# A graph-attention layer on one core: the last group of rows closed over three tiles and written out by itself

## What is computed

```python
h = jnp.maximum(_layernorm(x, axis=-1), 0.0)
h = h @ W.T                                   # 4096 x 256
src, dst = h @ a1, h @ a2
e = jax.nn.leaky_relu(src[:, None] + dst[None, :], negative_slope=0.2)
e = jnp.where(adj == 0, NEG_INF, e)           # adj is 4096 x 4096
out = x + jax.nn.softmax(e, axis=1) @ h
```

## Time and profile before

| what | value |
|---|---|
| median of three runs | 390.85 us |
| lowest and highest | 390.27, 391.11 us |
| profiled execution, its own time | 390.91 us |
| its span, first to last instruction | 389.3 us |
| mean granted TensorE clock | 1.000 of full speed |

### The profile page before, as it was taken

The page is one execution under the profiler, slowest core; times in us unless marked ns, Lnnn a source line. Parts: engine busy times, 40 slices in busy tenths (PEclk is TensorE's granted clock), DMA queues, the critical chain, the costliest instruction groups (busy, mean ns, idle before and its releaser), DMA issues.

```text
span 389.3 us, 9291 instructions
## 1 busy us (share of the span) xinstructions
PE 380.9 (98%) x3368; PEld 330.9 (85%) x3368; DVE 367.0 (94%) x476; ACT 196.7 (51%) x282; POOL 43.4 (11%) x73
## 2 busy tenths in 40 slices
PE   6999899999999999999999999999999999999996
PEld 5788588888888888888888888888888888888885
DVE  4999999999999999999999799999988999999965
ACT  5899956553345643444445543444345543444330
POOL 2898002000000001110000001100000011100000
PEclk9999999999999999999999999999999999999999
DMA  8920177876559567776666567766665567776403
GB/s 254 372 78 3 38 245 221 272 226 232 176 172 293 181 212 225 240 229 219 223 215 219 174 217 230 237 222 220 216 207 178 165 215 243 228 222 223 152 0 108
DMA packets 26108, 77.89 MB, mean 200 GB/s; under 512 B 2916, under 2 KB 8552, under 8 KB 26088
## 3 DMA queue, kind: packets, MB, share of 16 engines
q1 hardware_dynamic: 24528, 74.20, 58.9%
q0 software_dynamic: 1280, 3.16, 2.2%
q10 hardware_dynamic: 280, 0.26, 0.2%
HBM read 73.40 MB, written 4.21 MB: 199 GB/s over the span
## 4 chain that ended last, share of the span: by engine, by line
PE 87%; DVE 8%; ACT 2%; issue 1%; DMA 1%; SPq 0%; ACTq 0%; DVEq 0%
PE ps L1278 86%; DVE stats L733 2%; DVE hnt_lo L752 1%; DVE v_sb L765 1%; DMA x_sb<-x 1%; DVE rows_sb L1128 1%; DVE moments L737 1%; ACT c_row L493 0%; DVE first_lo L752 0%; ACT h_sb L465 0%; ACT hn_sb L472 0%; DVE hn_sb L760 0%; ACT hnt_hi L482 0%; PE ps L1216 0%; DVE shift L747 0%
## 5 line engine op out<-in xcount | busy, mean ns | idle before, releaser
L1278 PE MATMUL ps<-v_sb,p_hi 128*128 (+2 forms) x2048 | 252.8, 272 | 1.4 <-ACT p_hi L503 1.4
L513 ACT ACTIVATE p_hi<-p_sb,gp 128x1024 f16<-128x1024 f32 x126 | 144.4, 1149 | 167.7 <-DVE p_sb L793 138.8
L1278 PEld LDWEIGHTS ps<-v_sb,p_hi 128*128 128x128 f16 x2048 | 198.3, 97 | 30.1 <-ACT p_hi L503 1.5
L800 DVE SCALAR_TENSOR_TENSOR p_lo<-p_sb,gp,p_hi 128x1024 f16<-128x1024 f32 x126 | 160.3, 1275 | 9.0 <-ACT p_hi L513 8.8
L793 DVE SCALAR_TENSOR_TENSOR p_sb<-c_row,gp,adj_sb 128x1024 f32<-128x1024 uint32 (+1 forms) x126 | 160.1, 1275 | 0.0
L1278 PE MATMUL ps<-v_sb,p_lo 128*128 (+1 forms) x1024 | 141.3, 273 | 0.0
L1278 PEld LDWEIGHTS ps<-v_sb,p_lo 128*128 128x128 f16 x1024 | 99.6, 97 | 13.5 <-DVE p_lo L786 0.3
L449 POOL DMA_DIRECT2D out<-rows_sb x24 | 13.0, 541 | 260.8 <-DVE rows_sb L1095 260.8
L390 POOL TENSOR_SCALAR hn_sb<-x_sb,moments,rstd 128x256 f32<-128x256 f32 x17 | 21.0, 1241 | 8.4 <-DVE rstd L742 8.1
L1216 PE MATMUL ps<-ident,hn_sb 128*128 128x128 f32 x64 | 12.9, 293 | 1.8 <-ACT hn_sb L472 1.8
L733 DVE BATCH_NORM_STATS2 stats<-x_sb 128x6 f32<-128x256 f32 x32 | 12.4, 406 | 1.3 <-DMA x_sb<-x 1.3
(11 more groups left out here) (96 smaller groups left out, 113.6 us busy)
## 6 DMA issues: line engine op xcount, KB each, us to landing
adj_sb<-adj_t SPq DMA_DIRECT2D x128, 512.0 KB, 4.7
x_sb<-x SPq DMA_DIRECT2D x7, 512.0 KB, 8.8
out<-rows_sb POOLq DMA_DIRECT2D x24, 128.0 KB, 4.7
c_row<-c_flat SPq DMA_DIRECT2D x3, 512.0 KB, 5.6
out<-rows_sb SPq DMA_DIRECT2D x8, 128.0 KB, 1.8
x_sb<-x SPq DMA_DIRECT2D x2, 256.0 KB, 4.7
w_nat<-w SPq DMA_DIRECT2D x1, 256.0 KB, 2.8
w_f<-w_t ACTq DMA_DIRECT2D x1, 256.0 KB, 4.2
```

The costliest lines, as they stand in the source:

```text
L513: nc.scalar.activation(p_hi[:, u % R, :], p_sb[:, u % R, :], ACT.Copy, scale=p_scale[:, bass.ds(t, 1)])\
L800: nc.vector.scalar_tensor_tensor(out=p_lo[:, u % R, :], in0=p_sb[:, u % R, :], scalar=p_scale[:, bass.ds(t, 1)], in1=p_hi[:, u % R, :], op ...
L1278: return nc.tensor.matmul(ps[:, k, 0:width], part[:, u % R, k * P:(k + 1) * P], v_sb[:, bass.ds(t, 1), v, 0:width], start=start, stop=stop ...
```

## The change

Three things change. In the last group `last_sums` takes three tiles (29, 30, 31) instead of two, so that a block takes nine matmuls. TensorE's loop over the groups ends after group 2, and the last group's code is written out behind it. The wait for the low parts stands in front of each tile's first product in the first block, not once ahead of all; that holds for the closing sums of every group. VectorE takes the eight blocks of the last group as (0,1), (2,3), (4,5), (6), (7) instead of four pairs.

```diff
+    CLOSING = 3
+    ROWS_TOGETHER = ((0, 2), (2, 4), (4, 6), (6, 7), (7, 8))
...
-            for k in range(0, RB, 2):
-                b = (NG - 1) * RB + k
-                dve.wait_ge(rows_done, b + 2)
-                link(nc.vector.tensor_scalar(den[:, b:b + 2], ps[:, k:k + 2, F], den_scale[:, 0:1], DEN_TINY,
+            for k, k1 in ROWS_TOGETHER:
+                b, b1 = (NG - 1) * RB + k, (NG - 1) * RB + k1
+                dve.wait_ge(rows_done, b1)
+                link(nc.vector.tensor_scalar(den[:, b:b1], ps[:, k:k1, F], den_scale[:, 0:1], DEN_TINY,
                                              ALU.mult, ALU.max))
-                link(nc.vector.reciprocal(inv_den[:, b:b + 2], den[:, b:b + 2]))
+                link(nc.vector.reciprocal(inv_den[:, b:b1], den[:, b:b1]))
                 if k == 0:
                     dve.wait_ge(rows_free, (NG - 1) * RB + RB)
-                for n in (0, 1):
+                for n in range(k1 - k):
...
             def last_sums(t, n, closing):
 
-                pe.wait_ge(p_lo_ready, n + U)
                 for k in range(RB):
                     for u in range(U - closing, U):
+                        if k == 0:
+                            pe.wait_ge(p_lo_ready, n + (u + 1))
                         product(u, t + u, k, p_hi, 0, False, False)
...
-            def tiles(g, q, first, last):
+            def tiles(g, q, first, last, closing=2):
                 n = g * T + q * U
-                for u in range(U - 2 if last else U):
+                for u in range(U - closing if last else U):
                     sums(u, q * U + u, n, g, first and u == 0)
                 if last:
-                    last_sums(q * U, n, 2)
-
-            def group(g):
+                    last_sums(q * U, n, closing)
+
+            def group(g, closing):
                 tiles(g, 0, True, False)
                 with pe.Fori(1, Q - 1) as q:
                     tiles(g, q, False, False)
-                tiles(g, Q - 1, False, True)
+                tiles(g, Q - 1, False, True, closing)
...
-            with pe.Fori(1, NG) as g:
-                group(g)
+            with pe.Fori(1, NG - 1) as g:
+                group(g, 2)
+            group(NG - 1, CLOSING)
```

## The result

The changed kernel took 390.07 us, median of 8 runs (389.83 to 390.32), the kernel before beside it 391.20 (8 runs, 390.23 to 391.62). The ratio is 0.9979, 95% interval 0.9969 to 0.9989: 0.8 us faster by the centre of the interval, 0.4 to 1.2 by its ends. That lies on the bound of 0.2% that the prediction used.

The account below looks back on a forecast made before the run. The prediction took TensorE's matmul stream and the work after its last matmul as the bound. Its terms, -0.29 + 0 + 0 = -0.29 us, took the median from 390.85 to 390.56, rounded 390.6 us, range 390.1 to 391.2.

Parts of the forecast that it names:

- the bound of 0.2%: Whole kernel: a measurement can tell about 0.2%, 0.78 us, from no change; the expected gain was 0.07%.
- The stream holds: TensorE's matmuls: none added or removed, so the last still starts at 385.18 us if TensorE never waits.
- this sign: TensorE's last matmul: still at 385.2 us; the forecast is wrong if it moves by more than 0.1 us.
- The blocks' times and VectorE's backlog: Closing blocks: 0.994 us each; pair holds VectorE 1.25, single 0.85; block 7 starts 0.11 late, gain 0.29 us.
- The better bound of 0.40: End of VectorE's work: block 7 starts on time, gain 0.40 us, median 390.45; as a rival, chance 0.15.
- The waits tile by tile: Closing sums: waits before each tile's first product cost nothing; one wait on top would lose 0.31 us.
- The written-out group: Last group's code: 576 more matmuls of program, fetches hidden under the matmul stream; cost taken as 0.
- The rival of a second fetch: TensorE's jump back near 215.7 us: loop start fetched again, slower by 1.5 to 4.4 us; chance 0.05.
- One argument against it: Queue q8, 130 to 215 us: five packets spread over the whole 85 us, so fetches run with execution.
- Both branches hang on the last output: Kernel's end: last store and flag's branch both follow the last output; moving its start moves the end equally.
- the silent term of nothing for what lies outside of the changed stretch: Start and time outside the span: no change counted; 390.91 us with span 389.3 becomes 390.62 with 389.0.
- The chance of 0.90 for "no change": Verdict on the runs: faster 0.03, no change 0.90, slower 0.07.

Follow-up runs that it names:

- the longer branch: The kernel before with a wait and two small VectorE operations added in a branch that is not taken; ratio 1.0000 (0.9988 to 1.0011).
- one wait on top: The changed kernel with the one wait for tile 31's low part back ahead of the closing sums; ratio to the kernel before 0.9986 (0.9973 to 0.9998).
- flag later: The changed kernel with the reduction of the denominators done three times; ratio to the kernel before 1.0003 (0.9992 to 1.0015).
- the second kernel with this order: The changed kernel with all four last blocks single and the transposed weights loaded ahead of a1 and a2; ratio to the kernel before 1.0014.

## Why the prediction was right, and where it was off

- **The stream holds: right.** From the first sum to the last matmul it is 340.49 us in both profiles. The prediction put the last matmul at 385.2 us from the span's start, and called itself wrong if it moved by more than 0.1. It stands at 384.83, 0.35 sooner, and so does every row from group 1 on. By its letter this sign came; but it moved with the start, ahead of any changed instruction. The sign should have been a distance between two events and not a place.
- **The blocks' times and VectorE's backlog: right.** The prediction put block 6 to start 1.25 us after the pair 4, 5 and the last output 0.29 us sooner. Measured: 384.40 - 383.15 = 1.25, and 0.32. The term that was mis-sized is the small operations of a single block, taken as 0.26 from start to start after the 128x2 form; the 128x1 form takes 0.24 (384.40 to 384.64). So block 6 held VectorE for 0.84 us instead of 0.85, and block 7's output came 0.44 after its start instead of 0.46: together the missing 0.03. The better bound of 0.40 was reached with all four last blocks single (0.41).
- **The waits tile by tile: right.** They saved a stall that the prediction put at 0.31 us and that measured 0.34 in the weight loads, 0.24 in the stream. With three tiles the part is there 0.39 us in time (0.35 by the prediction), with four it is 2.00 us late.
- **The written-out group: right, nothing.** The rival of a second fetch didn't come: groups 1 and 2 start 84.80 us apart, and no packet of q8 came between 215 and 300 us. What such a fetch would cost, estimated from the landings of other transfers, no run shows. One argument against it was drawn too wide: the five packets of the first pass did not come over the whole 85 us. In the trace three lie between 130 and 164 us, none between 164 and 198, and two behind that.
- **"Both branches hang on the last output": right, and it hid something.** The flag's branch ends the span. Its start moved by the 0.35 of the start and 0.31 more (387.39 to 386.73).
- **The size in the runs: off.** The forecast of 390.6 us moved the median of the runs by the profile's difference and took the rest as scatter about a fixed place. The step that failed is the silent term of nothing for what lies outside of the changed stretch: the time outside of the span, and the start. Time less span fell from 1.65 to 1.53 us (the mean of the five runs with five groups of blocks and nothing more, 1.51 to 1.56; 1.51 in the changed kernel's own). That this can come from VectorE's program text alone is shown by the longer branch (1.52 against 1.64). With the tail it makes 0.32 + 0.12 = 0.44 us, the lower end of the measured interval of 0.4 to 1.2. The rest came from the start. So that the median still reached the stated range is partly luck: the gain was 0.8 us and not 0.3. (Half of the seen 0.84 us on each side of the centres would have been 390.0 to 391.3, a little wider than the range stated.)
- **What of the start stays open.** Shown: in every profile the chain leads back to the landing of a first load, the span spreads by over 1 us in one and the same program (388.2 to 390.0 us in 34 runs of the kernel before) and with it the start, as the stream doesn't (340.49 and 340.50 us in the two profiles of it), and the start comes sooner neither with the longer code (written out only, ratio 0.9999) nor with VectorE's longer branch (1.0000). Taking the stream, the tail and the end of each profile off its mean span, the first sum started on average at 44.3 us in the changed kernel both times and with all singles, and at 44.5, 44.7 and 44.9 in the three sets of the kernel before. In the other variants it was 44.4 (singles, two tiles), 44.5 (three tiles, pairs; four tiles), 44.6 (one wait on top; flag later) and 44.8 (written out; longer branch), and 44.5 in the kernel before run again. It isn't a lucky draw of a few runs: the sum starts by about 44.5 us in 25 of the 28 runs of the changed kernel and of all singles, and in 35 of the 94 of the kernel before. Nor is it the change as such: with one wait on top it is 5 of 9, with the later flag 5 of 10, and both contain the three tiles, the singles and the written-out group. What in the exact program brings the early landings isn't settled; I had no experiment that holds the first landings fixed.

So the mechanism and its price were right. With the time outside of the span they make 0.44 of the measured 0.8 us. The chance of 0.90 for "no change" was too sure: a gain near 0.45 us needs only 0.33 us from the start to reach the bound of 0.78, and the centre of the measurement did.

## What to carry to other kernels

Where a producer hands blocks to a consumer behind it, the tail is the consumer's work on the last hand-over plus its backlog; making the last hand-over smaller only pays when blocks come more slowly than the consumer takes single ones (here every 0.99 us against 0.84; at 0.66 it cost 0.34 us). So widen the spacing and shrink the last piece together. A pair just ahead of the singles leaves a backlog: here it cost 0.09 to 0.10 us until blocks 4 and 5 were single too. When the closing part starts earlier, move each wait to the first use it guards, and check how far the part reaches before an input is truly late. For gains of a tenth of a per cent read the stretch of the trace that the change touches, from one fixed event to another: here it repeated to 0.01 us while the runs scattered by 1.5 and more. Check the start of several runs before a difference in their median is put down to the change.

## What was not expected of the hardware

- A load of 1 KB issued by ScalarE behind one of 256 KB landed 3.97 us after its issue (3.13 in the second kernel with this order), and the kernel became 1.3 us slower. Issued first, its consumer ran at 4.02 us instead of 6.44.
- A wait and two small operations that are never executed, added to VectorE's program, changed the time outside of the span by 0.12 us (1.64 to 1.52).
- Code written out for 576 matmuls and their weight loads cost nothing measurable (ratio 0.9999 by itself): four instruction packets, 0.07 MB in all, came under a running matmul stream. 84.78 and 84.68 us lie ahead of and behind the written-out group's first matmul, as before. The jump between groups 1 and 2 left 84.80 us, and no packet of q8 came behind it.
